# Turning the attention row sums: VectorE folds two running totals in 32x32 blocks

## The reference, cut to what matters

```python
xn = _layernorm(x, axis=-1)
q = _split_heads(xn @ q_w.T + q_b, 16) / math.sqrt(32)
k = _split_heads(xn @ k_w.T + k_b, 16)
v = _split_heads(xn @ v_w.T + v_b, 16)
scores = jnp.einsum('bhqd,bhkd->bhqk', q, k)
attn = jax.nn.softmax(scores, axis=-1)
ctx = jnp.einsum('bhqk,bhkd->bhqd', attn, v)      # then heads are joined again
attn_out = ctx @ out_w.T + out_b
h = xn @ weight @ aux_weight1 @ aux_weight2
return x + attn_out + jnp.tanh(h + bias)
```

## Time and profile before

| | us |
|---|---|
| median of 3 runs | 4175.6 |
| lowest and highest of them | 4172.01, 4176.85 |
| span of the profiled execution | 4167.9 |
| PE busy in it | 4078.0 (98%) |
| POOL busy | 3253.1 (78%) |
| DVE busy | 3127.0 (75%) |
| ACT busy | 2356.4 (57%) |

### The profile page before, as it was taken

One profiled execution on the slowest core, in us unless ns is written; L12 is line 12 of the kernel. 1 busy time (PEld: TensorE's weight loads), 2 busy tenths in 40 slices (PEclk: granted clock), 3 DMA queues, 4 the chain that ended last, 5 costly groups with the idle time before them and its releaser, 6 DMA issues.

```text
span 4167.9 us, 77711 instructions
## 1 busy us (share of the span) xinstructions
PE 4078.0 (98%) x21216; PEld 2490.3 (60%) x21216; DVE 3127.0 (75%) x5058; ACT 2356.4 (57%) x4515; POOL 3253.1 (78%) x1180
## 2 busy tenths in 40 slices
PE   8999999889999999999999999999999999999999
PEld 6888888645555555555555555555555555555467
DVE  4443334668888888888888888888888888888454
ACT  2221222157676666666676666666666767666621
POOL 1222222179999999999999999999999999999930
PEclk9999999999999999999999999999999999999999
DMA  4444445368878888888888888878888888888787
GB/s 169 162 161 160 151 160 166 122 141 174 172 165 176 176 175 176 171 172 175 173 174 178 177 170 173 171 168 175 176 177 173 175 172 171 176 176 174 154 260 263
DMA packets 246352, 722.11 MB, mean 173 GB/s; under 512 B 87392, under 2 KB 88416, under 8 KB 184544
## 3 DMA queue, kind: packets, MB, share of 16 engines
q0 software_dynamic: 55296, 402.68, 49.8%
q1 hardware_dynamic: 107648, 201.88, 14.2%
q10 hardware_dynamic: 83040, 113.01, 9.8%
HBM read 178.00 MB, written 136.31 MB: 75 GB/s over the span
## 4 chain that ended last, share of the span: by engine, by line
PE 53%; DMA 14%; issue 7%; ACT 3%; POOL 2%; ACTq 0%; POOLq 0%; SPq 0%; DVE 0%; DVEq 0%
PE sm_bank L948 16%; PE st_bank L964 16%; PE pv_bank L970 16%; DMA dma_sum<-pool_sum 10%; DMA dma_sum<-probs 3%; ACT probs L781 3%; PE sm_bank L235 3%; PE sm_bank L970 1%; POOL pool_sum L716 1%; PE st_bank L235 1%; POOL ctx_out L741 0%; DMA q_stack<-s_y 0%; PE sm_bank L957 0%; DMA q_stack<-max_row 0%; POOL dma_sum L727 0%
## 5 line engine op out<-in xcount | busy, mean ns | idle before, releaser
L862 DVE TENSOR_REDUCE part_max<-sm_bank 128x1 f32<-128x512 f32 x4016 | 2442.3, 678 | 412.3 <-PE sm_bank L948 406.0
L716 POOL TENSOR_TENSOR pool_sum<-pool_sum,probs 128x2048 f32<-128x2048 f32 x512 | 2504.9, 4892 | 16.7 <-ACT probs L781 0.9
L781 ACT ACTIVATE probs<-st_bank 128x512 f32<-128x512 f32 x3840 | 1959.4, 616 | 608.6 <-PE st_bank L964 580.6
L964 PE MATMUL st_bank<-q_stack,k_stack 97*128 97x512 f32 x4096 | 1648.4, 403 | 19.2 <-ACT probs L781 8.3
L948 PE MATMUL sm_bank<-k_stack,q_stack 96*128 96x512 f32 x4016 | 1655.1, 412 | 3.0 <-issue 2.7
L948 PEld LDWEIGHTS sm_bank<-k_stack,q_stack 96*128 96x128 f32 x4016 | 763.3, 190 | 550.7 <-DVE part_max L862 334.1
L964 PEld LDWEIGHTS st_bank<-q_stack,k_stack 97*128 97x128 f32 x4096 | 779.9, 191 | 274.8 <-ACT probs L781 128.0
L970 PE MATMUL pv_bank<-probs,v_pair 128*32 128x512 f32 x7680 | 936.0, 602 | 0.0
L970 PEld LDWEIGHTS pv_bank<-probs,v_pair 128*32 128x32 f32 x7680 | 204.9, 110 | 455.7 <-ACT probs L781 262.9
L727 POOL DMA_DIRECT2D dma_sum<-probs x320 | 348.3, 1088 | 70.7 <-ACT probs L781 26.2
L356 POOL TENSOR_TENSOR y_out<-y_out,x_in 128x512 f32<-128x512 f32 x64 | 82.6, 1291 | 406.9 <-ACT y_out L388 401.1
(11 more groups left out here) (100 smaller groups left out, 2431.4 us busy)
## 6 DMA issues: line engine op xcount, KB each, us to landing
dma_sum<-probs POOLq DMA_DIRECT2D x320, 1024.0 KB, 8.3
dma_sum<-pool_sum POOLq DMA_DIRECT2D x64, 1024.0 KB, 10.3
q_stack<-s_q_hi ACTq DMA_DIRECT2D x122, 256.0 KB, 6.6
k_stack<-s_k_hi ACTq DMA_DIRECT2D x122, 256.0 KB, 4.8
x_in<-in_x SPq DMA_DIRECT2D x16, 1024.0 KB, 7.7
s_q_hi<-qk_hi SPq DMA_DIRECT2D x16, 1024.0 KB, 4.3
s_q_lo<-qk_lo SPq DMA_DIRECT2D x16, 1024.0 KB, 6.5
s_k_hi<-qk_hi SPq DMA_DIRECT2D x16, 1024.0 KB, 4.3
```

The source lines that it names most:

```text
L716: nc.gpsimd.tensor_tensor(total[:], one[:], tile_at(r, kt)[:], ALU.add).then_inc(pool_added, 1)
L781: nc.scalar.activation(tile_at(r, kt)[:, q * BLK:(q + 1) * BLK], st_bank[:, st_place(kt * QB + q)], ACT.Exp, scale=SCALE).then_inc(probs_r ...
L862: nc.vector.tensor_reduce(part_max[:, k:k + 1], sm_bank[:, sm_place(k)], AX.X, ALU.max).then_inc(max_scores_read, 1)
L964: nc.tensor.matmul(st_bank[:, st_place(u)], k_st[r][0:ROWS + 1, kt * P:(kt + 1) * P], q_st[r][0:ROWS + 1, q * BLK:(q + 1) * BLK], start=Tr ...
```

## The change

- VectorE sums over 32 partitions: eight `TENSOR_REDUCE` instructions a head (`fold`), each over 128x512 of `pool_sum` or of `dma_sum`, with the input turned in 32x32 blocks. From 128x2048 of one total come 128x64 partial sums (`folded`). They stand after maximum units 30, 34, 38, 42 (for `pool_sum`) and 49, 53, 57, 61 (for `dma_sum`). The first of each four waits for its total.
- `merge` is gone. The two totals are folded apart.
- The pass of `ones` over 512 columns is gone. `add_up` has eight matmuls of 16 columns against `pick` (a 128x32 matrix that repeats the 32x32 identity four times). It stands after pair 5 (`CUT = 12`) where it stood after pair 4, and its place in `SM_TURN` is behind unit 63 where it was behind unit 55.
- `copy_sums` and `recip` are gone. VectorE inverts 128x16 straight from the bank (`invert`, ahead of maximum unit 0) and spreads the result over 128x512 with one block transpose (`spread_out`, after unit 3). TensorE's maximum unit 1 waits for `invert`.
- Tile 14 moves to the DMA chain, which is now 0, 2, 4, 7, 9, 13, 14: six joins, the last of them (join 6) behind the next head's first add, where `merge` stood. GpSimd has nine tiles and eight adds. `scale` stands ahead of its eighth add.
- In the weights stage GpSimd builds `pick` with a memset and four selects in place of the memset of `ones`.

```diff
...
-SUM_UNIT = 56
-RECIPS = [63, 7, 15]
-CUT = 10
+SUM_UNIT = 64
+POOL_FOLDS, DMA_FOLDS = [30, 34, 38, 42], [49, 53, 57, 61]
+INVERT, SPREAD = 0, 3
+CUT = 12
...
-CHAINS = [[0, 2, 5, 8, 10, 13]]
-MERGE_AFTER = 0
+CHAINS = [[0, 2, 4, 7, 9, 13, 14]]
+LAST_AFTER = 0
 POOL_TILES = [kt for kt in range(KT) if not any(kt in tiles for tiles in CHAINS)]
 POOL_ADDS = len(POOL_TILES) - 1
-JOINED = len(CHAINS[0]) * DMA
+JOINED = (len(CHAINS[0]) - 1) * DMA
 JOIN_AFTER = {1: 2, 3: 3, 5: 4, 7: 5}
-SLOT = {kt: i % 7 for i, kt in enumerate([*range(1, 13), 14, 15])} | {13: 7}
-SCALE_ADD = 8
-RESULT_TILES = [9, 11]
+SLOT = {kt: i % 7 for i, kt in enumerate([*range(1, 14), 15])} | {14: 7}
+SCALE_ADD = 7
+RESULT_TILES = [8, 10]
...
-            nc.gpsimd.memset(keep["ones"][:], 1.0)
+            nc.gpsimd.memset(keep["pick"][:], 0.0).then_inc(pick_ready, 1)
...
+            for b in range(QB):
+                pool.wait_ge(pick_ready, b + 1)
+                nc.gpsimd.affine_select(out=keep["pick"][:], in_=keep["pick"][:], compare_op=ALU.not_equal, fill=1.0,
+                                        base=-b * DH, pattern=[[-1, DH]], channel_multiplier=1).then_inc(pick_ready, 1)
...
-            def merge(h, r):
-
-                pool.wait_ge(pool_added, PRIME + h * POOL_ADDS + POOL_ADDS)
-                pool.wait_ge(joined[r % 2], landed(h, len(CHAINS[0]) - 1))
-                pool.sem_inc(join_due, 1)
-                nc.gpsimd.dma_start(dma_sum[r % 2][:], pool_sum[r % 2][:], accum_op=ALU.add).then_inc(joined[r % 2], DMA)
-
             def scale(h, r):
                 pool.wait_ge(pv_copied, PRIME + h + 1)
-                pool.wait_ge(recip_ready, h * len(RECIPS) + len(RECIPS))
+                pool.wait_ge(recip_ready, h + 1)
...
-                    if i == MERGE_AFTER:
-                        merge(h, r)
+                    if i == LAST_AFTER:
+                        join(h, r, len(CHAINS[0]) - 1)
...
-                        if kt == CUT - 1:
-                            copy_sums(h, r)
...
-            def recip(h, r, piece):
-
-                if piece == 0:
-                    dve.wait_ge(sums_copied, PRIME + h + 1)
-                    dve.wait_ge(context_ready, PRIME + h)
-                cut = [BLK // len(RECIPS) // 8 * 8 * i for i in range(len(RECIPS))] + [BLK]
-                columns = slice(cut[piece], cut[piece + 1])
-                nc.vector.reciprocal(ratio[:, columns], sum_copy[r % 2][:, columns]).then_inc(recip_ready, 1)
+            def fold(h, r, part, piece):
+
+                if part == 0 and piece == 0:
+                    dve.wait_ge(pool_added, PRIME + h * POOL_ADDS + POOL_ADDS)
+                if part == 1 and piece == 0:
+                    dve.wait_ge(joined[r % 2], landed(h, len(CHAINS[0]) - 1))
+                total = (pool_sum, dma_sum)[part][r % 2][:, piece * BLK:(piece + 1) * BLK]
+                blocks = slice(piece * (BLK // DH), (piece + 1) * (BLK // DH))
+                nc.vector.tensor_reduce(folded[r % 2][:, part, blocks], total.rearrange("p (b j) -> p b j", j=DH), AX.X,
+                                        ALU.add, apply_transpose=True).then_inc(fold_ready, 1)
+
+            def invert(h):
+                dve.wait_ge(sums_ready, PRIME + h + 1)
+                nc.vector.reciprocal(inverse[:], sum_bank).then_inc(sums_read, 1)
+
+            def spread_out(h):
+                dve.wait_ge(sums_read, PRIME + h + 1)
+                dve.wait_ge(context_ready, PRIME + h)
+                nc.vector.transpose(ratio[:].rearrange("p (b j) -> p b j", j=DH),
+                                    inverse[:].unsqueeze(2).to_broadcast([P, BLK // DH, DH])).then_inc(recip_ready, 1)
...
+                if sums_of is not None and k == INVERT:
+                    invert(sums_of[0])
...
-                if k in RECIPS and sums_of is not None:
-                    recip(*sums_of, RECIPS.index(k))
+                if sums_of is not None:
+                    for part, places in enumerate((POOL_FOLDS, DMA_FOLDS)):
+                        if k in places:
+                            fold(*sums_of, part, places.index(k))
+                    if k == SPREAD:
+                        spread_out(sums_of[0])
...
-                    for piece in range(len(RECIPS)):
-                        recip(h, r, piece)
+                    for part in range(2):
+                        for piece in range(QB):
+                            fold(h, r, part, piece)
+                    invert(h)
+                    spread_out(h)
...
-                    pe.wait_ge(sums_copied, PRIME + s - 1)
+                    pe.wait_ge(sums_read, PRIME + s - 1 - back)
...
-                pe.wait_ge(joined[r % 2], landed(h, len(CHAINS[0])))
-                spread(sum_bank, ones[:], dma_sum[r % 2], True, True).then_inc(sums_ready, 1)
+                pe.wait_ge(fold_ready, h * (2 * QB) + 2 * QB)
+                width = BLK // DH
+                for q in range(QB):
+                    for part in range(2):
+                        last = nc.tensor.matmul(sum_bank[q * DH:(q + 1) * DH, :], pick[:],
+                                                folded[r % 2][:, part, q * width:(q + 1) * width], start=part == 0,
+                                                stop=part == 1)
+                last.then_inc(sums_ready, 1)
...
```

29 lines of the change are left out of this document (13 added, 16 removed).

## The result

| | before | after |
|---|---|---|
| median of 4 runs, us | 4173.81 (4167.79 to 4176.85) | 4230.11 (4218.89 to 4233.09) |
| profiled span, us | 4167.9 | 4230.9 |
| one head, value pass to value pass, us | 48.72 | 49.64 |

The ratio after to before is 1.0123, with a 95% interval of 1.0106 to 1.0139 (the two medians of the table by themselves give 1.0135). The kernel became 1.2% slower. The forecast was 4214 with a range of 4138 to 4260. A head was forecast 0.62 us longer; in the mean of 55 heads it is 0.92 longer. The two spans differ by 63 us. Of these, 51.0 lie in the 63 periods from the first value pass over pair 0 to the last (the last heads of the changed kernel are shorter than its mean), 5.2 in the remaining pairs of the last head, 6.3 behind the last value pass and 0.5 ahead of the first. The ends were forecast at nothing.

The account below looks back on a forecast made before the run. TensorE was taken as the bound, at 48.75 us a head. The terms summed to +0.62 us a head, +39 us over 63 heads on 4167.9, plus 7.7 from span to median: 4214 us, range 4138 to 4260.

Parts of the forecast that it names:

- The ends: First and last heads: `pick` in GpSimd's idle time, last folds beside the last stage's matmuls; nothing for both.
- sum pass and `invert`: After the pairs' scores: sum pass 0.75 for 1.0, -0.25 us a head; maximum unit 1 waiting for `invert`, +0.15.
- three reciprocals go: VectorE: their lag cost pair 0 its 0.12, so removing them gives -0.10 us a head.
- folds in pairs 2, 3, 4: VectorE's folds ahead of the fourth maximum: +0.07 in pair 2, +0.40 each in pairs 3 and 4, +0.87 a head.
- join 6 at pair 4: VectorE awaits this DMA ahead of the fold behind unit 49, TensorE behind it: +0.45 us a head.
- Lag behind the fourth maximum is paid: A 0.60 fold ahead of a pair's fourth maximum costs TensorE 0.40; behind the fourth, lag is free.
- rival of the free lag: VectorE's lag costs TensorE nothing: -0.70 us a head, 4131 us, or 4157 with one 0.40 left; chance 0.20.
- second walk: Turning needs a second walk over a fold's input: 1.2 us a fold, some +4.5 a head, 4450 us; chance 0.05.
- The rival in which it lands in time: Join 6 costs no wait and the parts cancel: +0.17 us a head, some 4176 to 4184; chance 0.20.
- An add less on GpSimd: worth nothing directly: GpSimd: some 5 us less work a head; no TensorE wait names an add, so no gain is counted.
- the exponentials' 0.35 hides it: Pairs 2 and 5: TensorE's waits for exponentials give 0.35 slack, hiding fold lag but for 0.07 and 0.
- A join 6 that takes 11.5: Rival of a very late join 6: landing over 11.5 us, a head +1.4 and more, 4265 us; chance 0.07.

Follow-up runs that it names:

- e9: Changed kernel with GpSimd and DMA sharing tiles as before (five joins, nine adds), `dma_sum` folded first, all folds at other units: 4199.1 us, ratio 1.0064 to before.
- e11: e9 plus join 4 held until VectorE has written the row of maxima, folds at 36, 39, 44, 47 and 52, 55, 59, 60: 4130.4 us, ratio 0.9889.
- e7: Kernel before without its merge, GpSimd's ten tiles left out of the denominator: 4219.3 us against 4177.5, ratio 1.0108.
- e10: e5 with GpSimd issuing join 4 only once VectorE has written the next head's row of maxima: 4157.2 us, ratio 0.9953 to before.
- e5: Changed kernel without join 6, tile 14 left out of the sum: 4250.4 us, ratio 1.0181 to before.
- e12: Changed kernel whole, with join 4 issued only once the next head's row of maxima is written: 4224.5 us against 4178.5 before, ratio 1.0112.
- e1: Changed kernel with every fold moved behind the fourth maximum of its pair: 4243.3 us against 4180.0 before, ratio 1.0158.
- e4: Changed kernel with tile 5 in the DMA chain in place of tile 4: 4229.5 us, ratio 1.0134 to before.
- e13: e11 with folds spread: `pool_sum` behind units 28, 31, 36, 39, `dma_sum` behind 44, 52, 59, 60: 4368.5 us against 4176.3 before, ratio 1.0453.

## Why the prediction was right in its sign, and where its steps were not

The terms per head. "Measured" is worked out from the table of intervals. For pair 5 without a sum pass I take 6.14, between the 6.12 of e9 and e11 and the 6.15 to 6.19 of pairs of its kind.

| term | forecast | measured | from |
|---|---|---|---|
| wait for the merge goes | -0.50 | -0.55 | e7: 7.57 to 7.02 |
| sum pass and `invert` | -0.10 | -0.43 | before 7.02 - 6.14 = 0.88; after 6.24 - 5.79 = 0.45 |
| three reciprocals go | -0.10 | -0.18 | pairs 7 and 0 without them, e10: 5.80 and 5.79 |
| folds in pairs 2, 3, 4 | +0.87 | +0.77 | 0.04, 0.33, 0.40 |
| join 6 at pair 4 | +0.45 | +0.59 | e5: 6.78 to 6.19 |
| pair 5, tile 4's buffer and lowered clock | 0 | +0.39 | 6.53 - 6.14 |
| row of maxima at pair 0 | 0 | +0.33 | 6.12 to e12's 5.79 |
| sum | +0.62 | +0.92 | 49.64 - 48.72 |

**Lag behind the fourth maximum is paid, 0.40 of 0.60.** Right, and the best supported of the steps: 0.40 in pairs 3 and 4 of e5, none of it in e1 where the folds stand behind the fourth., one instruction in two pairs, were enough for it. The small error is in the base: pair 3 took 5.86 before and not 5.78, so only 0.33 was added. The rival of the free lag is refuted, as is that of the second walk (0.62 a fold).

**Join 6 takes the merge's place.** Right in mechanism and place, and near in size in its own pair: issued 16.7 into the head for a forecast 16.0, a VectorE wait of 0.47 a head for a forecast 0.5, and 0.59 of TensorE's time for 0.45. What it sets off in pairs 5 and 0 was not in the sum. The rival in which it lands in time is refuted.

**The sum pass was mis-sized.** I had taken 0.75 between bounds of 0.43 and 1.7, and another 0.15 for `invert`. Both together cost 0.45. The sixteen instructions are over in 0.33, under even the lower bound of 0.43; some 0.12 is left for `invert` and for the lag of VectorE. I had also counted the old pass at its full 1.0 where the interval gave back 0.88. A third of a microsecond a head too dear, 21 us over 63 heads.

**The reciprocals** were costed in pair 0 alone, though `RECIPS` has three places, and the one behind unit 7 lengthens pair 7 as the one behind unit 15 lengthens pair 0: 5.89 and 5.88 before.

**Two terms were missing, and both begin with a transfer.** "An add less on GpSimd: worth nothing directly" is the step that failed. With less to do, GpSimd issues join 4 sooner, 2.0 us in the mean, and where the row is late behind the wait for join 6 as well, it comes behind the join: in 20 of 55 heads, +0.33. The trace of before had it: the row was sent 2.33 us ahead of that join, and I took some 5 us off the engine that issues the join. And the fold term took pair 5 at 0 "as the exponentials' 0.35 hides it", without asking what else can hold TensorE in it. Of its 0.39, 0.19 is the clock that is lowered behind join 6's wait, in 7 of 55 heads; without join 6 (e5) there is none in this pair. The rest is tile 4's place in the chain, which has its buffer wanted again by tile 11 before join 2 has read it: with tile 5 in its place (e4) the heads at full clock fall from 6.36 to 6.19. The few hundredths that are left are the fold behind unit 57.

**The ends were taken at nothing.** They cost 12.0 us: 0.5 ahead of the first value pass over pair 0 and 11.5 behind the last. Which of folds, join 6 and spreading it is no run shows.

**How near the time came is luck in part.** Inside a head the missing terms (+0.72) and the ones taken too dear or too cheap (-0.42 net: -0.05, -0.33, -0.08, -0.10, +0.14) offset in part. Over the 63 periods that left 51.0 for a forecast 39, and the ends added their 12, so the profiled span was forecast 24 us too short. The median of the runs then lay 0.8 below the profiled span, where I had put it 7.7 above. So the time is 16 us off, while single steps of a head, over 63 heads, were off by 21 to 25. The sign leans on the missing terms too. Folds and join 6 are the two largest costs, as forecast, but by the terms that were in the sum a head is only 0.92 - 0.72 = 0.20 longer, 13 us over 63 heads.

Three of the rivals' sums don't come out, and none decided anything. +0.17 a head is 11 us, so 4186 for the cancelling parts and not 4176 to 4184. A join 6 that takes 11.5 waits 1.7 by my own count, +1.9 a head and not 1.4. And 1.4 in three pairs and 1.0 in a fourth are 5.2 a head for the second walk, not 4.5.

What stays open is why join 6 lands late, and the row with it, in mostly every fourth head. The heads use their buffers in groups of four, which would give that period, but no run changed it.

## What to carry to other kernels

Taking work or a wait off an engine that isn't the bound moves its DMAs earlier: list every transfer it issues with the small, urgent ones of other queues beside it, and write down which is ahead by how much. The work you take off may be what keeps the order; where it goes, put the order in by a semaphore (e10: 1.41 us a head). A wait of about 1 us on the engine that is the bound can cost more than itself when the clock is lowered behind it: read the granted clock of the stretch that follows before you put its length down to something else. Extra work on an engine that closely follows the bound is free only behind the instruction whose buffer comes round next, and what is gained in one pair has to be looked for in the next ones, since a chain of transfers which has its own pace takes it back (e1).

## What the runs showed of the hardware that I had not expected

- A DMA of 8 KB that is issued 1.06 us behind a 1 MB accumulating DMA lands in 6.83 us; issued 0.57 ahead of one it lands in 1.8. In e5, where it is nearly always behind, its median is 6.8.
- A sum over 32 partitions in turned blocks, 128x512 in float32, costs VectorE 0.62 us in a row of instructions, where a plain maximum over the same shape costs 0.60, and 0.70 by itself.
- Sixteen matmul instructions of 16 columns, each with its load of 32 columns, are over in 0.33 us.
- Behind a wait of 1.29 us TensorE's granted clock was 0.53 for 3.41 us, and a value pass took 3.47 us for 1.92. In the changed kernel that came in 7 of the 13 heads with a wait of 1.0 us or more for join 6, in e13 in 43 of 55 heads.
- Leaving work out made two kernels slower than with it: e5 than the changed kernel (4250 against 4230), e7 than the one before (4219 against 4178).
